# Preactivation convolutions with a mixture block, one core: the order of stores, halos, scales and PSUM banks in the last four steps

## The chip, the cores and the metric

The kernel runs on one core of one Trainium2 chip. The metric is the device time of one execution in microseconds (us), median of three: 566.34 us (565.69 to 567.6). Differences of about 0.3% (1.7 us) or less can't be told from no change here.

## The reference, cut to what matters

Four layers, each added to its input; the group norm has 4 groups of 2 channels over the whole image, so no element of a layer can be normalised before the last of its image is known.

```python
# x: (4, 8, 256, 256) float32: four images of eight channels
def _gn(v, G=4, eps=1e-05):
    g = v.reshape(B_, G, C_ // G, H_, W_)
    m = jnp.mean(g, axis=(2, 3, 4), keepdims=True)
    s = jnp.var(g, axis=(2, 3, 4), keepdims=True)
    return ((g - m) / jnp.sqrt(s + eps)).reshape(v.shape)
x = x + _L0_conv_ref(_gn(x), L0_conv_weight, L0_conv_bias)     # 3x3 convolution, 8 to 8 channels, padding 1
x = x + _L1_conv_ref(_gn(x), L1_conv_weight, L1_conv_bias)
x = x + _L2_conv_ref(_gn(x), L2_conv_w1, L2_conv_b1, L2_conv_w2, L2_conv_b2)
#   h = gelu(einsum('bend,edf->benf', x, w1) + b1); einsum('benf,efd->bend', h, w2) + b2, one pair of matrices per channel
x = x + _L3_conv_ref(_gn(x), L3_conv_weight, L3_conv_bias)
```

## The kernel before, in words

**Tiling.** An image is held as 128 partitions (column parity, channel, row within a band of 8) by 4096 columns (32 bands of 128 column pairs), in float32 in `X`. It is worked on in 8 chunks of 512 columns, one PSUM bank each. The convolutions are twelve steps: 0 to 3 the first layer on images 0 to 3, 4 to 7 the second, 8 to 11 the last (images 0 to 3). The gated matrices (L2) lie between step 7 and step 8.

**One step of a convolution.** GpSimd (`scale_and_bias`) turns the image's variance into a scale and a bias per partition. ScalarE (`normalise_piece`) writes the normalised piece twice: as float16 into `XN` and as float32 into `SCR`; GpSimd (`low_part`) subtracts the two into the low half of `XN`. An image has five pieces (2, 2, 1, 1, 2 chunks). The rows above and below a band belong to other partitions, so DMAs copy them from `XN` to `HALO`: for each half of an image four transfers of `halo_columns` and four of `halo_thirds`. TensorE computes the part within a band (`centre`, 3 matmuls for each chunk) and then, for four chunks at a time, the sides and halos (`tiles`: 48 matmuls on quarters of the array, in two halves of 24, first those signalled as `cross_mm`, then those as `conv_mm`). VectorE adds the bank to `X` (`conv_update`). The four `conv_update`s of a half of an image in the last layer give output, stored by DMAs from `X` to `out`.

**Statistics.** The means and variances within a partition come from VectorE (`bn_stats`, `bn_aggr`). Across the partitions of a group, two tiny TensorE matmuls sum them: `group_mean(n)`, then VectorE's `deviation(n)`, then `group_variance(n)`, then VectorE's `variance(n)`, which lets GpSimd make the scale. The last layer has n = 12 to 15 for images 0 to 3.

**The last layer.** The results of the matrices for images 2 and 3 are transposed on TensorE (`results(b, first, last)`) and added by VectorE (`mlp_chunk`) in the same stretch in which steps 8 and 9 run, so that image 3's statistics are complete only within step 9. The order on each engine is written out by hand; there is no scheduler. `ORDER` lists in which order the chunks of `X` become final, and semaphore waits are counted from it. `L3_BANKS` gives the PSUM bank of each of the 32 chunks of the last layer. `XN` and `HALO` have three slots; step 11 uses the slot of step 8. SP and ScalarE each have a DMA queue, which they fill in program order: whatever SP waits for, all its later transfers wait too.

## Time and profile before

| | |
|---|---|
| time, median of 3 | 566.34 us (565.69 to 567.6) |
| the profiled execution | 566.28 us |
| its span, first to last instruction | 564.5 us |
| TensorE busy, share of the span | 515.9 us, 91% |
| VectorE, ScalarE, GpSimd busy | 372.4 us, 295.7 us, 170.5 us |
| moved by DMA | 57.41 MB, mean 102 GB/s |
| output written | 8.39 MB |

The span is 1.8 us shorter than the time of its execution; the rest lies around it. A busy share is a mean over the whole program. In the last 45 us it says little: there the engines take turns, and it counts which wait ends last. Times in the rows below are microseconds from the span's start. In a timeline each row is an instruction or several merged ones; what stands in brackets is how long the engine was idle before it and what ended that.

### The profile page before, as it was taken

How to read it: one execution, taken by the hardware profiler on the slowest of the kernel's cores; microseconds unless marked ns; L12 is line 12 of the kernel's file. 1: busy time of each engine (PE TensorE's matmuls, PEld its weight loads, DVE VectorE, ACT ScalarE, POOL GpSimd, SP SyncE). 2: the span in 40 equal slices, each digit the busy share in tenths (PEclk: the TensorE clock that was granted, in tenths of full speed). 3: DMA queues.
4: the chain of work that ended last, by engine and by line, in shares of the span. 5: the costliest groups of instructions: out<-in, count | busy, mean ns of one | idle time of the engine just before them, and what ended most of it. 6: DMA issues, size and time to landing. Idle time of an engine off the chain costs nothing.

```text
span 564.5 us, 9154 instructions
## 1 busy us (share of the span) xinstructions
PE 515.9 (91%) x3374; PEld 259.3 (46%) x3374; DVE 372.4 (66%) x637; ACT 295.7 (52%) x363; POOL 170.5 (30%) x188
## 2 busy tenths in 40 slices
PE   0779999996989999999999999999999989998874
PEld 0434444563544444444444444444444445864431
DVE  4889999987866394194193293292358388898523
ACT  2699988553734453353353362352346646886430
POOL 4679888886470000000000000000000000587430
PEclk9799999997899999999999999999999999999988
DMA  8845655543020221021022012012132300054778
GB/s 318 345 109 144 155 136 137 134 124 150 1 75 1 75 75 75 0 74 74 0 74 74 2 73 74 10 64 74 35 115 75 138 12 2 1 133 109 241 229 330
DMA packets 14168, 57.41 MB, mean 102 GB/s; under 512 B 3116, under 2 KB 3244, under 8 KB 11052
## 3 DMA queue, kind: packets, MB, share of 16 engines
q1 hardware_dynamic: 12396, 51.39, 28.5%
q10 hardware_dynamic: 1740, 5.58, 2.8%
q8 instruction: 21, 0.34, 0.3%
q14 instruction: 11, 0.09, 0.0%
HBM read 30.03 MB, written 8.39 MB: 68 GB/s over the span
## 4 chain that ended last, share of the span: by engine, by line
PE 61%; DVE 16%; ACT 7%; POOL 5%; DMA 3%; SPq 3%; issue 3%; ACTq 0%; DVEq 0%; POOLq 0%
PE PS L1097 26%; PE PS L1071 25%; DVE X L735 6%; DVE ST L696 5%; PE PS L973 3%; SPq L262 3%; POOL XN L384 3%; ACT SCR L494 2%; ACT XN L489 2%; PE PS L1028 2%; DMA X<-x 2%; DMA HALO<-XN 2%; PE PS L1127 2%; PE PS L966 1%; DVE SM L711 1%
## 5 line engine op out<-in xcount | busy, mean ns | idle before, releaser
L1071 PE MATMUL PS<-XT,W1S 128*128 (+1 forms) x768 | 171.7, 382 | 2.8 <-POOL XT L433 2.5
L1097 PE MATMUL PS<-HID,W2S 128*128 128x512 f16 x720 | 159.5, 379 | 1.6 <-DVE W2S L760 1.6
L535 ACT ACTIVATE SCR<-PS,CONST 128x512 f32<-128x512 f32 x128 | 87.2, 687 | 64.5 <-PE PS L1071 28.0
L1071 PEld LDWEIGHTS PS<-XT,W1S 128*128 128x128 f16 x768 | 75.5, 99 | 92.2 <-issue 5.9
L1097 PEld LDWEIGHTS PS<-HID,W2S 128*128 128x128 f16 x720 | 70.4, 98 | 82.9 <-issue 1.8
L384 POOL TENSOR_TENSOR XN<-SCR,XN 128x1024 f16<-128x1024 f32 (+1 forms) x61 | 100.5, 1671 | 24.3 <-ACT SCR L494 24.1
L760 DVE SCALAR_TENSOR_TENSOR W2S<-W2F,W2S 128x2048 f16<-128x2048 f32 x10 | 22.9, 2291 | 114.6 <-ACT W2S L531 114.6
L361 POOL MEMSET XN<- 128x128 f16 x6 | 2.8, 460 | 304.3 <-PE PS L1097 304.0
L696 DVE BATCH_NORM_STATS2 ST<-X 128x6 f32<-128x512 f32 x128 | 81.6, 682 | 9.4 <-DMA X<-x 8.2
L489 ACT ACTIVATE XN<-X,SC 128x1024 f16<-128x1024 f32 (+1 forms) x61 | 64.2, 1052 | 32.1 <-POOL SC L375 23.2
L973 PE MATMUL PS<-XN,CWT 64*64 64x512 f16 x288 | 68.5, 385 | 8.1 <-DMA HALO<-XN 8.1
L735 DVE SCALAR_TENSOR_TENSOR X<-PS,X 128x512 f32<-128x512 f32 x96 | 59.6, 680 | 22.9 <-PE PS L988 22.9
L966 PE MATMUL PS<-XN,CWT 128*128 128x512 f16 x288 | 68.8, 385 | 2.8 <-DVE X L735 1.4
L807 DVE SCALAR_TENSOR_TENSOR HID<-SCR,HID 128x512 f16<-128x512 f32 x96 | 67.4, 702 | 3.3
L986 PE MATMUL PS<-HALO,CWT 49*64 49x512 f16 (+1 forms) x288 | 68.9, 385 | 0.0
L988 PE MATMUL PS<-HALO,CWT 49*64 49x512 f16 (+1 forms) x288 | 68.9, 385 | 0.0
L975 PE MATMUL PS<-XN,CWT 64*64 64x512 f16 x288 | 68.5, 385 | 0.0
L494 ACT ACTIVATE SCR<-X,SC 128x1024 f32<-128x1024 f32 (+1 forms) x61 | 64.1, 1050 | 2.5 <-POOL XN L384 1.9
L561 ACT ACTIVATE YT<-PS,CONST 128x512 f32 (+1 forms) x24 | 16.5, 688 | 88.7 <-PE PS L1097 88.7
L804 DVE TENSOR_SCALAR HID<-SCR 128x512 f16<-128x512 f32 x96 | 40.8, 425 | 9.5 <-ACT SCR L535 6.4
L973 PEld LDWEIGHTS PS<-XN,CWT 64*64 64x64 f16 x288 | 29.3, 108 | 37.5 <-DMA HALO<-XN 11.0
L966 PEld LDWEIGHTS PS<-XN,CWT 128*128 128x128 f16 x288 | 27.3, 100 | 36.8 <-issue 4.8
(52 smaller groups left out, 482.4 us busy)
## 6 DMA issues: line engine op xcount, KB each, us to landing
W1F<-w SPq DMA_DIRECT2D x10, 1024.0 KB, 4.8
W2F<-w SPq DMA_DIRECT2D x10, 1024.0 KB, 4.8
HALO<-XN SPq DMA_DIRECT2D x48, 129.9 KB
HALO<-XN SPq DMA_DIRECT2D x48, 121.8 KB
X<-x SPq DMA_DIRECT2D x2, 2048.0 KB, 18.8
out<-X ACTq DMA_DIRECT2D x8, 512.0 KB, 5.2
HALO<-XN SPq DMA_DIRECT2D x42, 64.9 KB
HALO<-XN SPq DMA_DIRECT2D x42, 60.9 KB
```

The lines of the kernel that those rows point to most:

```text
L384: pool.tensor_tensor(XN[s][:, 1, rows, 1:NJ + 1], SCR[:, m % 2, 0:n * CH].rearrange("p (t j) -> p t j", j=NJ), XN[s][:, 0, rows, 1:NJ + 1] ...
L489: act.activation(XN[s][:, 0, i * TC:(i + n) * TC, 1:NJ + 1], src.rearrange("p (t j) -> p t j", j=NJ), ACT.Identity, bias=SC[:, k, 1:2], sc ...
L494: act.activation(SCR[:, m % 2, 0:n * CH], src, ACT.Identity, bias=SC[:, k, 1:2], scale=SC[:, k, 0:1]).then_inc(xn_ok, 1)
L535: act.activation(SCR[:, ft % 2, 0:CH], bank(ft % G_RING), ACT.Gelu, bias=BT[:, ds(e * FT + ft, 1)], scale=1.0 / (XS * WS)).then_inc(gelu_o ...
L696: dve.bn_stats(ST[:, n % 4, slot], src).then_inc(bn_ok, 1)
L735: dve.scalar_tensor_tensor(out=xc, in0=bank(conv_bank(q)), scalar=1.0 / (XS * WS), in1=xc, op0=ALU.mult, op1=ALU.add).then_inc(x_new, 1)
L966: pe.matmul(to, CWT[:, w, l, 0:P], XN[s][:, part, rows, 1:NJ + 1], start=(n == 0), stop=False)
L973: odd = pe.matmul(bank(k, HALF_P, P), CWT[0:HALF_P, w, l, SIDE:EDGE], XN[s][0:HALF_P, part, rows, 2:NJ + 2], start=False, stop=last)
L986: even = pe.matmul(bank(k, 0, HALF_P), CWT[0:kh, w, l, EDGE:CWN], HALO[s][0:kh, part, rows, 0:NJ], start=False, stop=last)
L988: odd = pe.matmul(bank(k, HALF_P, P), CWT[HALF_P:HALF_P + kh, w, l, EDGE:CWN], HALO[s][HALF_P:HALF_P + kh, part, rows, 0:NJ], start=False, ...
L1071: mm = pe.matmul(bank(ft % G_RING), W1S[:, w, h * NF + ft * P:h * NF + (ft + 1) * P], rhs, start=(n == 0), stop=(n == 3 * DH - 1))
L1097: mm = pe.matmul(bank(G2_BANK + h), W2S[:, w, ft * NW + h * P:ft * NW + (h + 1) * P], HID[slot][:, part, ft], start=(ft == 0 and part == 0 ...
```

## The change

It touches the last four steps alone. On SP, stores (512 KB transfers from `X` to `out`) now stand between the halo transfers: two of image 0 between the two halves of step 9's halos and two behind them, then step 10's halos, then four stores of image 1 and two of image 2, then step 11's halos. ScalarE no longer issues image 0's stores; it issues the thirds of step 10 (`last_thirds(10, ...)`) and those of step 11 after all five pieces of the step, and image 2's second half and part of image 3's stores at the end. GpSimd makes image 2's scale (`scale_and_bias(14)`) before the last piece of step 9. On TensorE the sums of n = 14 and 15 are issued in the middle of `tiles`, and the last two results of image 3 come earlier. VectorE takes up the last result of image 3 after two of step 9's updates. `L3_BANKS` uses up to eight banks.

```diff
-L3_STAT_BANK = 2
+L3_STAT_BANK = (2, 6)
-L3_BANKS = [(3, 4, 5, 0, 1)[n % 5] for n in range(2 * NCH)]
-L3_BANKS += [(6, 7, 4, 5, 0, 1, 3)[n % 7] for n in range(2 * NCH)]
+L3_BANKS = [3, 4, 5, 0, 1, 3, 4, 5, 0, 1, 2, 3, 4, 5, 0, 1]
+L3_BANKS += [(7, 6, 2, 3, 4, 5, 0, 1)[n % 8] for n in range(2 * NCH)]
-THIRDS_BY_ACT = ((0, 0), (11, 0), (11, 1),)
+THIRDS_BY_ACT = ((0, 0), (10, 0), (10, 1), (11, 0), (11, 1))
@@ SP
-        for g in range(8, 11):
-            load_ones(SLOT[g])
-            halos(g)
-        for i in range(0, NCH, 2):
-            sp.wait_ge(x_new, X_NEW_AT["c", 9, i + 1])
-            sp.dma_start(out[1][:, i * CH:(i + 2) * CH], x_chunk(1, i, 2)
-                         ).then_inc(out_done, 16)
+        def store(b, i, n=2):
+            sp.wait_ge(x_new, X_NEW_AT["c", 8 + b, i + n - 1])
+            sp.dma_start(out[b][:, i * CH:(i + n) * CH], x_chunk(b, i, n)).then_inc(out_done, 16)
+        def store_half(b, i):
+            store(b, i)
+            store(b, i + 2)
+        load_ones(SLOT[8])
+        halos(8)
+        load_ones(SLOT[9])
+        halos(9, lambda: store_half(0, 0))      # called between the two halves of the halos
+        store_half(0, QUAD)
+        load_ones(SLOT[10])
+        halos(10)
+        store_half(1, 0)
+        store_half(1, QUAD)
+        store_half(2, 0)
         halos(11)
-        for i in range(NCH):
-            sp.wait_ge(x_new, X_NEW_AT["c", 11, i])
-            sp.dma_start(out[NB - 1][:, i * CH:(i + 1) * CH], x_chunk(NB - 1, i)
-                         ).then_inc(out_done, 16)
+        store(NB - 1, 0)
+        store(NB - 1, 4, 1)
+        store(NB - 1, 6, 1)
@@ GpSimd
-        low_parts(9)
+        low_parts(9, 0, 4)
+        scale_and_bias(14)
+        low_parts(9, 4)
...
-        for g in range(10, 12):
-            scale_and_bias(g + 4)
-            low_parts(g)
+        low_parts(10)
+        scale_and_bias(15)
+        low_parts(11)
@@ ScalarE
-        for g in range(9, 11):
+        for g in range(9, 12):
             normalise(g)
-        store(0)
-        slot_free(11)
-        for k in range(4):
-            normalise_piece(FIRST_PIECE[11] + k)
-        last_thirds(0)
-        normalise_piece(FIRST_PIECE[11] + 4)
-        last_thirds(1)
-        store(2)
+            if g >= 10:
+                last_thirds(g, 0)
+                last_thirds(g, 1)
+        store(2, 4)
+        store(2, 6)
+        store(NB - 1, 2)
+        store(NB - 1, 5, 1)
+        store(NB - 1, 7, 1)
@@ TensorE, banks of the last layer
-                elif L3_BANKS[n] >= TR_BANK:
-                    pe.wait_ge(x_new, X_NEW_AT["y", 3, 6 + L3_BANKS[n] - TR_BANK])
+                elif L3_BANKS[n] in L3_STAT_BANK:
+                    pe.wait_ge(var_ok, 2 * (15 + L3_STAT_BANK.index(L3_BANKS[n])))
+                elif L3_BANKS[n] == TR_BANK + 1:
+                    pe.wait_ge(x_new, X_NEW_AT["y", 3, NCH - 1])
@@ TensorE, order
-        tiles(8, 0)
-        group_mean(14)
+        tiles(8, 0, lambda: group_mean(14))
...
-        tiles(9, 0)
-        results(3, 6, 6)
+        tiles(9, 0, lambda: results(3, 6, 6))
+        results(3, 7, 7)
         last_centres(9, 4, 7)
-        results(3, 7, 7)
-        tiles(9, QUAD, lambda: group_mean(15))
-        group_variance(15)
+        group_mean(15)
+        tiles(9, QUAD, lambda: group_variance(15))
```

On VectorE, in the first half of step 9's updates up to image 3's variance (L735, now L749, is a `conv_update`; L753, now L767, adds a result, and L696, now L710, takes its statistics; L701 to L719, now L715 to L733, are the aggregate, deviation and variance), before:

```order
L735 SCALAR_TENSOR_TENSOR X<-PS,X 128x512 x4
L753 TENSOR_TENSOR X<-PS,X 128x512
L696 BN_STATS ST<-X 128x6
L701 BN_AGGR MV<-ST 128x2
L707 TENSOR_TENSOR SM<-MV,PS 128x1
L709 TENSOR_SCALAR SM<-PS 128x1
L711 SCALAR_TENSOR_TENSOR SM<-SM,MV 128x1
L717 TENSOR_SCALAR SM<-PS 128x1
L719 TENSOR_SCALAR SM<-PS 128x1
L735 SCALAR_TENSOR_TENSOR X<-PS,X 128x512 x20
```

and now:

```order
L749 SCALAR_TENSOR_TENSOR X<-PS,X 128x512 x2
L767 TENSOR_TENSOR X<-PS,X 128x512
L710 BN_STATS ST<-X 128x6
L715 BN_AGGR MV<-ST 128x2
L749 SCALAR_TENSOR_TENSOR X<-PS,X 128x512
L721 TENSOR_TENSOR SM<-MV,PS 128x1
L723 TENSOR_SCALAR SM<-PS 128x1
L725 SCALAR_TENSOR_TENSOR SM<-SM,MV 128x1
L749 SCALAR_TENSOR_TENSOR X<-PS,X 128x512
L731 TENSOR_SCALAR SM<-PS 128x1
L733 TENSOR_SCALAR SM<-PS 128x1
L749 SCALAR_TENSOR_TENSOR X<-PS,X 128x512 x20
```

The last result of image 3 moved ahead of two of the four updates, which now stand where VectorE had nothing between the steps of the statistics.

On SP's queue, step 10's halos and what follows them (`HALO_57` is step 10's slot), before:

```order
L318 DMA HALO_57<-ones 2x4160 [waits zero_ok2]
L262 DMA HALO_57<-XN_56 16x2x1948 [waits zero_ok2,lo_ok,pads_ok2,conv_mm]
L262 DMA HALO_57<-XN_56 16x2x1948
L262 DMA HALO_57<-XN_56 16x2x2078 x2
L262 DMA HALO_57<-XN_56 8x2x1948 x2
L262 DMA HALO_57<-XN_56 8x2x2078 x2
L262 DMA HALO_57<-XN_56 16x2x2078 [waits lo_ok]
L262 DMA HALO_57<-XN_56 16x2x2078
L262 DMA HALO_57<-XN_56 16x2x1948 x2
L262 DMA HALO_57<-XN_56 8x2x2078 x2
L262 DMA HALO_57<-XN_56 8x2x1948 x2
L344 DMA out<-X 128x1024 [waits x_new] x4
```

and now (with the first of step 11's, `HALO_54`):

```order
L344 DMA out<-X 128x1024 [waits x_new] x2
L321 DMA HALO_57<-ones 2x4160 [waits zero_ok2]
L263 DMA HALO_57<-XN_56 16x2x1948 [waits zero_ok2,lo_ok,pads_ok2,conv_mm]
L263 DMA HALO_57<-XN_56 16x2x1948
L263 DMA HALO_57<-XN_56 16x2x2078 x2
L263 DMA HALO_57<-XN_56 16x2x2078 [waits lo_ok]
L263 DMA HALO_57<-XN_56 16x2x2078
L263 DMA HALO_57<-XN_56 16x2x1948 x2
L344 DMA out<-X 128x1024 [waits x_new] x6
L263 DMA HALO_54<-XN_52 16x2x1948 [waits zero_ok0,lo_ok,pads_ok0,conv_mm]
```

The eight transfers of eight rows have left this queue for ScalarE's, two stores stand ahead of step 10's halos, and six instead of four between them and step 11's.

## Rows read from the trace of the kernel before

**Rows 1.** Busy time by stretch; columns: stretch, its length, each engine, clock, DMA.

```profile
core 0: us, PE busy (x) PEld busy (x) DVE busy (x) ACT busy (x) POOL busy (x), PEclk, DMA share, GB/s
...
536.00:542.00 6.00, 6.00 (x64) 2.77 (x63) 3.02 (x6) 2.18 (x3) 3.56 (x3) 1.00 0.98 362
...
547.00:550.40 3.40, 3.40 (x36) 1.52 (x36) 0.00 (x0) 0.00 (x0) 0.25 (x1) 0.50 0.49 95
```

**Rows 2.** Timeline of TensorE, 519 to 566 us.

```profile
521.95 2.15 PE L966 MATMUL PS<-XN,CWT 128*128 128x512 f16 x9 [1.45 <-DVE X L735]
...
526.45 0.38 PE L931 MATMUL PS<-MV,CONST 128*128 128x1 f32 x2 [0.49 <-DVE MV L701]
...
528.44 2.79 PE L966 MATMUL PS<-XN,CWT 128*128 128x512 f16 x12
532.16 0.40 PE L973 MATMUL PS<-XN,CWT 64*64 64x512 f16 x1 [0.93 <-DMA HALO<-XN]
...
540.36 2.80 PE L966 MATMUL PS<-XN,CWT 128*128 128x512 f16 x12
546.88 0.56 PE L973 MATMUL PS<-XN,CWT 64*64 64x512 f16 x1 [3.72 <-DMA HALO<-XN]
...
551.29 2.80 PE L966 MATMUL PS<-XN,CWT 128*128 128x512 f16 x12
```

**Rows 3.** Timeline of VectorE, 506 to 559 us.

```profile
506.95 0.14 DVE L719 TENSOR_SCALAR SM<-PS 128x1 f32<-128x1 f32 x1
...
519.89 0.69 DVE L753 TENSOR_TENSOR X<-PS,X 128x512 f32<-128x512 f32 x1 [1.53 <-PE PS L1044]
...
524.57 0.69 DVE L753 TENSOR_TENSOR X<-PS,X 128x512 f32<-128x512 f32 x1 [0.88 <-PE PS L1044]
...
528.61 0.16 DVE L717 TENSOR_SCALAR SM<-PS 128x1 f32<-128x1 f32 x1 [1.26 <-PE PS L936]
...
556.29 2.48 DVE L735 SCALAR_TENSOR_TENSOR X<-PS,X 128x512 f32<-128x512 f32 x4 [2.97 <-PE PS L988]
```

**Rows 4.** Timeline of GpSimd, 507 to 525 us.

```profile
507.38 2.06 POOL L384 TENSOR_TENSOR XN<-SCR,XN 128x1024 f16<-128x1024 f32 x1 [1.03 <-ACT SCR L494]
...
511.09 0.56 POOL L368 TENSOR_TENSOR RS<-SM,RS 128x1 f32<-128x1 f32 x1
...
517.50 4.24 POOL L384 TENSOR_TENSOR XN<-SCR,XN 128x1024 f16<-128x1024 f32 x3 [0.18 <-ACT SCR L494]
522.78 2.06 POOL L384 TENSOR_TENSOR XN<-SCR,XN 128x1024 f16<-128x1024 f32 x1 [1.03 <-ACT SCR L494]
```

**Rows 5.** Timeline of ScalarE, 508 to 554 us.

```profile
512.78 1.25 ACT L489 ACTIVATE XN<-X,SC 128x1024 f16<-128x1024 f32 x1 [5.48 <-POOL SC L375]
...
530.60 1.25 ACT L489 ACTIVATE XN<-X,SC 128x1024 f16<-128x1024 f32 x1 [7.89 <-POOL SC L375]
```

**Rows 6.** Timeline of SP's queue, 505 to 562 us.

```profile
505.35 10.41 SPq L262 DMA_DIRECT2D HALO<-XN  x16
...
535.56 3.21 SPq L344 DMA_DIRECT2D out<-X  x4
538.93 11.08 SPq L262 DMA_DIRECT2D HALO<-XN  x8
```

**Rows 7.** The chain that ended last, 519 to 566 us.

```profile
520.77 0.61 SPq L262
...
522.40 2.39 SPq L262
...
529.70 2.42 DMA HALO<-XN
...
542.82 4.01 DMA HALO<-XN
```

**Rows 8.** All stores from X to out, by tile.

```profile
L349 SPq DMA_DIRECT2D out<-X x8: 332/1166/1218, 551.6 to 559.9; - x8
...
DMA to landing us min/median/max: 3.1/5.0/7.8
```

More of the change, by code:

```diff
@@ L89 @@
 ORDER += [("c", 8, i) for i in range(QUAD, NCH)] + [("y", 3, i) for i in range(3, 7)]
-ORDER += [("c", 9, i) for i in range(QUAD)] + [("y", 3, 7)]
-ORDER += [("c", 9, i) for i in range(QUAD, NCH)]
+ORDER += [("c", 9, 0), ("c", 9, 1), ("y", 3, 7)]
+ORDER += [("c", 9, i) for i in range(2, NCH)]
 ORDER += [("c", g, i) for g in range(10, 12) for i in range(NCH)]
@@ L190, in stat_psum @@
     def stat_psum(n, col):
-        k = 0 if n == 13 else L3_STAT_BANK if n > 13 else STAT_BANK
+        k = 0 if n == 13 else L3_STAT_BANK[n - 14] if n > 13 else STAT_BANK
         return PS[:, k * CH + col:k * CH + col + 1]
@@ L298, in _, with halos @@
         load_image(3, 0, NT, x3_in)
-        def halos(g):
+        def halos(g, between=None):
             s = SLOT[g]
@@ L309, in halos @@
                 halo_thirds(sp, s, 0, NT // 2, halo_a[s])
+            if between is not None:
+                between()
             sp.wait_ge(lo_ok, PIECE_OF[g, NCH - 1] + 1)
@@ L338, in _ @@
             load_w2(e)
-        for g in range(8, 11):
-            load_ones(SLOT[g])
-            halos(g)
-        for i in range(0, NCH, 2):
-            sp.wait_ge(x_new, X_NEW_AT["c", 9, i + 1])
-            sp.dma_start(out[1][:, i * CH:(i + 2) * CH], x_chunk(1, i, 2)
-                         ).then_inc(out_done, 16)
-        halos(11)
-        for i in range(NCH):
-            sp.wait_ge(x_new, X_NEW_AT["c", 11, i])
-            sp.dma_start(out[NB - 1][:, i * CH:(i + 1) * CH], x_chunk(NB - 1, i)
-                         ).then_inc(out_done, 16)
-        sp.wait_ge(out_done, 16 * (NPR * (NB - 1) + NCH))
+        def store(b, i, n=2):
[14 more added lines that the diff above has]
+        store_half(2, 0)
+        halos(11)
+        store(NB - 1, 0)
+        store(NB - 1, 4, 1)
+        store(NB - 1, 6, 1)
+        sp.wait_ge(out_done, 16 * (NPR * NB + 2))
     @block.gpsimd
@@ L664, in _, with store, last_thirds @@
             last_result(1, dh)
-        def store(b):
-            for i in range(0, NCH, 2):
-                act.wait_ge(x_new, X_NEW_AT["c", 8 + b, i + 1])
-                act.dma_start(out[b][:, i * CH:(i + 2) * CH], x_chunk(b, i, 2)
-                              ).then_inc(out_done, 16)
-        def last_thirds(half):
-            s = SLOT[11]
+        def store(b, i, n=2):
+            act.wait_ge(x_new, X_NEW_AT["c", 8 + b, i + n - 1])
+            act.dma_start(out[b][:, i * CH:(i + n) * CH], x_chunk(b, i, n)
+                          ).then_inc(out_done, 16)
+        def last_thirds(g, half):
+            s = SLOT[g]
             act.wait_ge(pads_ok[s], 2)
             act.wait_ge(zero_ok[s], 4)
-            act.wait_ge(conv_mm, 2 * NCH * (HAD[11] + 1))
-            act.wait_ge(lo_ok, PIECE_OF[11, NCH - 1 if half else QUAD] + 1)
+            act.wait_ge(conv_mm, 2 * NCH * (HAD[g] + 1))
+            act.wait_ge(lo_ok, PIECE_OF[g, NCH - 1 if half else QUAD] + 1)
             halo_thirds(act, s, half * NT // 2, (half + 1) * NT // 2, (halo_a, halo_b)[half][s])
-        for g in range(9, 11):
+        for g in range(9, 12):
             normalise(g)
-        store(0)
-        slot_free(11)
-        for k in range(4):
-            normalise_piece(FIRST_PIECE[11] + k)
-        last_thirds(0)
-        normalise_piece(FIRST_PIECE[11] + 4)
-        last_thirds(1)
-        store(2)
+            if g >= 10:
[6 more added lines that the diff above has]
+        store(NB - 1, 7, 1)
     @block.vector
@@ L908, in _ @@
             mlp_chunk(3, i)
-        last_updates(9, 0, None)
+        conv_update(9, 0)
+        conv_update(9, 1)
         mlp_chunk(3, 7)
         aggregate(15)
+        conv_update(9, 2)
         deviation(15)
+        conv_update(9, 3)
         variance(15)
@@ L928, in group_mean @@
                 pe.wait_ge(yt_ok, 4 * NE + 2)
+            elif n == 15:
+                pe.wait_ge(x_new, X_NEW_AT["y", 3, 6])
             elif n >= 1:
```

## The prediction

> **What bounds the kernel now.** I read four views. The busy time by stretch comes first: nothing that the change touches lies ahead of 502 us, so only the last 62 us can move. TensorE is at full clock there except from 547.0 to 550.4 us, where the granted clock is 0.50, its lower level of 1.2 GHz; just before that it had stood idle [rows 1, 2]. The timeline of TensorE then shows which waits it has: 1.45 us for an update by VectorE (a PSUM bank is not free), 0.49 us for image 3's aggregate, 0.93 us for the first halos of step 10 and 3.72 us for the first halos of step 11 [rows 2]. Everything between them is matmuls back to back: four `centre`s take 2.73 us and a full `tiles` as much (from 532.16 to 540.36 there are three such blocks and no gap [rows 2]). Third, who is late behind the halos: ScalarE sits idle 5.48 us before step 10 and 7.89 us before step 11, each time for the scale [rows 5]. GpSimd makes image 2's scale at 511.09, only after the last piece of step 9 (507.38) [rows 4], though VectorE had the variance at 507.1; it can make image 3's only after VectorE has read that variance at 528.61 [rows 3]. Fourth, the queue: SP issues a halo transfer every 0.65 us (16 in 10.41 us) when the DMA engines are free [rows 6], but 2.39 us for one when 2 MB of stores run beside it [rows 7]. Before step 11 its four stores of image 1 (2 MB) go ahead of the halos; these start at 538.93 (the stores at 535.56), TensorE gets them at 546.88, 7.95 us later, with the DMA engines 98% busy from 536 to 542 [rows 1, 2, 6]. After the last update ends (556.29 + 2.48 = 558.77) the span runs another 5.7 us on stores [rows 3].
>
> **The change part by part.** I carry the starts of instructions, since matmul ends overlap.
>
> Step 8. The mean of image 2 moves into `tiles`. It has to wait there for the aggregate by some 0.5 us; but TensorE waited about as long afterwards for VectorE's deviation, which doesn't move. I take 0; from -0.3 to +0.5 (the 0.49 of the same kind of wait [rows 2]).
>
> Step 9, TensorE. Chunk (9,5) took bank 0 from (9,0), whose update VectorE began only after the result (3,6). With bank 2 put in, (9,6) is the first chunk to need it, one `centre` (0.69) later; and the result (3,6) comes half a `tiles` (1.3 us) earlier, so VectorE can begin it at about 518.5 instead of 519.89 [rows 3] and (9,0) at 519.8 instead of 521.2. TensorE reaches (9,6) at 521.6, so that wait goes, 1.45 us, 1.5 with the refilling of the pipeline. The aggregate: 518.5, plus 1.3 for the result and its statistics, 1.25 for two updates and 1.83 for the last result, its statistics and the aggregate (524.57 to the mean's matmul at 526.45 [rows 2, 3], less its start) gives 522.9. TensorE gets to the mean at 522.9 as well, so the second wait (0.49, with the refilling 0.6) goes too. Step 10's centres begin 2.1 us earlier, at 526.3. Bounds: 0.6, if the bank wait only moves to the mean, to 2.3.
>
> Image 3's scale. The variance's matmul is now in the middle of `tiles`, at 523.0 + 0.3 + 1.3 = 524.6; VectorE reads it 0.4 later, at 525.0, against 528.61 [rows 3]. The two updates that stand between don't delay it: the deviation waits for the mean until 523.4 and one update (0.6) fits on each side. GpSimd is free by then, so everything behind the scale moves 3.6 us: ScalarE starts step 11 at 527.0 instead of 530.60 [rows 5].
>
> Image 2's scale. It goes ahead of step 9's last piece, so it can start once GpSimd has piece four and the variance, at 507.2 (506.95 + 0.14 [rows 3]; piece four is done at 506.4, where GpSimd's idle 1.03 us begin) instead of 511.09. It takes 1.7 us, from 511.09 to ScalarE's start at 512.78 [rows 4, 5]. What it pushes back is that piece (507.38 to 509.1), the memsets behind it, and step 9's second halos by 0.6 us; TensorE needs these only at 523, and SP issues them by 519 (below). ScalarE starts step 10 at 509.1 instead of 512.78. GpSimd is busy with the delayed piece (2.06) and 1.6 us of memsets (509.4 to 511.0 now) until 512.8 and passes on 2.5 us of it: the piece that step 10's first halos wait for (the second of three at 517.50 [rows 4]) is ready at 518.2 instead of 520.7, the last at 522.3 instead of 524.8.
>
> SP's queue. Step 9's first eight halos end at 510.6 as now. Two stores (1 MB) cost 1.3 us to issue, the eight second halos 5.2 us plus 1.1 for the stores beside them (beside 2 MB eight issues, the first at 520.77 and the last at 529.70, took 8.9 us between them instead of 7 x 0.65, 4.3 more [rows 7]; I take a quarter of that for half the data, and a half as the bound). Two more stores and the ones: 520.2. Step 10's four column halos, 2.5 + 1.1 us, are issued by 523.8 and land by about 526.3 (the last one's issue to landing was 2.42 us [rows 7]). The four thirds, which leave this queue, go out on ScalarE's at 518.1 to 521. TensorE wants them at 526.3 + 2.73 = 529.0. So the wait of 0.93, 1.0 with the refilling, goes, with 2.7 us to spare. Of the stores, image 1's are out by 530; image 2's first two wait for updates at 532.5 and 533.7.
>
> Step 11's halos. SP began them at 538.93, as soon as the piece was ready; 3.6 to 3.9 us earlier is 535.0 to 535.3. SP has just issued the second of image 2's stores and reaches the halos at 535.1; 1 MB is ahead of them instead of 2 MB, and ScalarE issues its thirds at the same time and not before a piece that it still has to normalise. Four issues with 1.1 extra begin the last at 538.1 (now four from 538.93 begin the last at 542.82, 3.89 us [rows 6, 7]; this is 3.0); at 2.42 us for landing it is there at 540.6. TensorE is ready at 526.3 + 5 x 2.73 = 540.0. I take a wait of 0.6 us instead of 3.8 with the refilling, a gain of 3.2. Bounds: no wait (gain 3.8), or 7.95 us from start to landing as now, 543.1, a wait of 3.1 (gain 0.7).
>
> Clock. The first `tiles` of step 11 took 546.88 to 551.29, 4.41 us instead of 2.73, since 3.4 us of it ran at 0.50 [rows 1, 2]. Waits of 1.45 and 0.93 us left the clock at 1.00 and 3.72 us did not. With 0.6 us I count the 1.7 us as gained; all of it stays lost if the wait is near 3.7.
>
> End. Of image 3's second half, SP and ScalarE each issue two 256 KB stores; now SP issues eight in a row at 1.17 us each, the last at 559.9, 1.2 us after its update was done [rows 3, 8]. Also 2 MB of image 2 no longer drains at the same time; only 1 MB of it, 6 us earlier. The last store now took 4.1 us to land; the least of all stores is 3.1 us [rows 8]. I take 3.7: 5.7 becomes 0.05 + 3.7 + 0.4 = 4.15, a gain of 1.6; bounds 1.2 and 2.2.
>
> The Trainium skill (Trainium Kernel Development and Optimization, Key Constraints) says that DMAs from SP and ScalarE run on the same 16 engines and that issuing from several only saves the sequencer's issue time. By that rule alone the end would give 1.2 us and not 1.6, and the sum would be 557.0. This trace has both queues busy at once in its last 10 us and can't tell saved issue from saved transfer.
>
> **The sum.** 2.1 (step 9) + 1.0 (step 10's halos) + 3.2 (step 11's) + 1.7 (clock) + 1.6 (end) = 9.6 us. The profiled execution took 566.28, which is the median of 566.34 but for 0.06: 566.3 - 9.6 = 556.7; I forecast **556.7 us**, a span of 554.9. Its own range is 554.6 to 559.0.
>
> **The rivals.**
>
> A. The stores hold the halos as long as now. What counts is then not the 2 MB but that stores stand directly ahead on one queue: step 11's halos take the 7.95 us again, land at 543.1, TensorE waits 3.1 us and its clock falls as now. 2.5 us and 1.7 us of the gain are lost: 560.9. For it: the landing took 4.01 us behind 2 MB [rows 7], and six stores now stand ahead of these halos. Against it: four of them will have drained.
>
> B. A halo's completion follows all earlier stores. A store takes up to 7.8 us to land [rows 8]; if the halos' signal can't be earlier than that of the store issued at 533.7, it comes at 541.5 to 542, 1.2 us after my value: 557.9. The Trainium skill (DMA: Bandwidth & Descriptors, Queues, rings and completion order) has such a rule: the semaphore increment lands only after every earlier write of its DMA engine, across queues. By it ScalarE's queue would be no way round the stores. The trace has no halo landing before a store issued ahead of it that it could be held against.
>
> C. Image 3's scale is no earlier: VectorE, not TensorE, is the bound of step 9, and the updates put between the statistics cost what they save. The variance stays near 528; halos of step 11 start at 538.9 on empty queues, land at 543.4: 561.2. Against it are VectorE's three gaps of 1.53, 0.88 and 1.26 us there [rows 3].
>
> D. Slower. SP is one chain now: step 10's halos behind four stores. If the stretched prices hold for each (8.9 + 0.6 us for the eight second halos of step 9, 3.9 + 0.9 for four of step 10, 4.0 to land [rows 6, 7]) they come at 532.7 instead of 526.3. Past 532.1, today's arrival, nothing is won there; TensorE idles 3.8 us and loses 1.7 us of clock; update (10,3) and so image 2's second store move to 539.7, and step 11's halos, queued behind that store, take their 7.95 us from 541: 549.0, against 546.88 now, with the clock lost again. Less 1.6 at the end: 567 to 568. It takes all prices at their worst at once.
>
> E. The halos keep TensorE waiting as before and only the end is gained: 564.7 to 566, within 0.3%.
>
> **How the numbers follow.** Forecast 0.62, A 0.17, B 0.09, C 0.05, D 0.04, E 0.03. The range from 554.6 to 561.3 leaves out D, E and the tails of the others, together about 0.15. 0.3% is 1.7 us, about what a measurement tells from no change. Faster: all of the first four, 0.93; same, E and a share of D, 0.03; slower 0.04.
>
> **What would show it.** TensorE: no wait before the three centres of step 9, step 10's centres at 526 and its `tiles` at 529 with no idle time, step 11's first `tiles` at 540 to 541 after under 1.5 us, no stretch at 0.50 before the last update. GpSimd: scale of image 2 at 507.2, of image 3 at 525 to 525.5. SP: step 10's first halo at 520 to 521, step 11's at 535. Last update's end to span's end: 4.2 us. I am wrong if a wait of over 3 us for halos remains in step 10 or 11, if image 3's scale begins after 527, or if the end still takes 5.7 us.

## The result, and the profile after

The changed kernel takes 556.38 us (median of 4, 555.54 to 560.05) against 566.36 us (565.69 to 567.6, 4 runs) of the kernel before on the same chip: a ratio of 0.9829, 95% interval 0.9803 to 0.9855, or 9.98 us faster. The forecast was 556.7 us. The profiled execution took 555.82 us with a span of 554.0 us, against 566.28 and 564.5. One execution of run 9 below (1091.39 us) and one of the kernel before beside runs 1 to 4 (1091.97 us) took about twice as long as all others and are in no ratio.

TensorE's timeline from 515 us on, to be laid beside [rows 2]:

```profile
520.18 2.79 PE L988 MATMUL PS<-XN,CWT 128*128 128x512 f16 x12
526.25 2.80 PE L988 MATMUL PS<-XN,CWT 128*128 128x512 f16 x12
531.72 2.80 PE L988 MATMUL PS<-XN,CWT 128*128 128x512 f16 x12
537.18 2.80 PE L988 MATMUL PS<-XN,CWT 128*128 128x512 f16 x12
541.04 0.40 PE L995 MATMUL PS<-XN,CWT 64*64 64x512 f16 x1 [1.05 <-DMA HALO<-XN]
543.77 2.80 PE L988 MATMUL PS<-XN,CWT 128*128 128x512 f16 x12
```

Of the four waits of before one is left, 1.05 us before step 11's first `tiles`. Step 10's centres start at 526.25 (528.44 before); from there to 537.18 blocks follow each other every 5.47 us, so the halos of step 10 are in time. VectorE, GpSimd and ScalarE around the two scales, beside [rows 3 to 5] (one fence for each engine):

```profile
519.71 1.27 DVE L749 SCALAR_TENSOR_TENSOR X<-PS,X 128x512 f32<-128x512 f32 x2
...
548.77 2.48 DVE L749 SCALAR_TENSOR_TENSOR X<-PS,X 128x512 f32<-128x512 f32 x4 [2.98 <-PE PS L1010]
```

```profile
506.96 0.56 POOL L381 TENSOR_TENSOR RS<-SM,RS 128x1 f32<-128x1 f32 x1 [0.82 <-DVE SM L733]
...
525.23 0.56 POOL L381 TENSOR_TENSOR RS<-SM,RS 128x1 f32<-128x1 f32 x1 [3.60 <-DVE SM L733]
```

```profile
508.64 1.24 ACT L504 ACTIVATE XN<-X,SC 128x1024 f16<-128x1024 f32 x1 [1.55 <-POOL SC L388]
...
526.91 1.24 ACT L504 ACTIVATE XN<-X,SC 128x1024 f16<-128x1024 f32 x1 [7.42 <-POOL SC L388]
```

Both scales start on VectorE's variance and on nothing else: image 2's at 506.96 (511.09 before), image 3's at 525.23; ScalarE starts step 11 at 526.91 instead of 530.60. SP's queue, beside [rows 6]:

```profile
518.02 1.09 SPq L344 DMA_DIRECT2D out<-X  x2
519.17 0.82 SPq L321 DMA_DIRECT2D HALO<-ones  x1
520.15 6.35 SPq L263 DMA_DIRECT2D HALO<-XN  x8
526.55 3.44 SPq L344 DMA_DIRECT2D out<-X  x4
532.57 1.53 SPq L344 DMA_DIRECT2D out<-X  x2
534.86 6.79 SPq L263 DMA_DIRECT2D HALO<-XN  x8
```

Image 1's 2 MB are issued from 526.55 to 530.0; the first of them stands eight microseconds before step 11's halos, the last some five. The DMA engines are far from idle in between. The next two lines show it, with the DMA share and GB/s as their last two numbers:

```profile
532.00:534.00 2.00, 2.00 (x11) 0.91 (x10) 1.73 (x3) 1.94 (x4) 2.00 (x2) 1.00 0.96 377
534.00:536.00 2.00, 2.00 (x33) 0.91 (x35) 0.00 (x0) 2.00 (x3) 1.86 (x2) 1.00 1.00 399
```

By the packets of the trace (those of 4,096 bytes are the stores' alone), image 1's stores end at 533.9 and image 2's first two at 537.4, after the first halo transfer of step 11 has been issued. Now the chain that ended last, beside [rows 7], and all stores, beside [rows 8]:

```profile
534.94 0.63 ACTq L263
...
536.30 0.70 ACTq L263
537.03 3.96 DMA HALO<-XN
541.04 0.40 PE PS L995
```

```profile
L344 SPq DMA_DIRECT2D out<-X x13: 332/430/1155, 510.4 to 550.7; - x13
L683 ACTq DMA_DIRECT2D out<-X x5: 338/338/1274, 542.1 to 551.3; - x5
...
DMA to landing us min/median/max: 2.2/4.3/6.2
```

Last, the busy time by stretch, beside [rows 1]: the granted clock is 1.00 where it was 0.50.

```profile
530.00:536.00 6.00, 6.00 (x78) 2.75 (x70) 2.48 (x4) 5.94 (x8) 5.67 (x4) 1.00 0.99 395
536.00:542.00 6.00, 4.95 (x56) 2.17 (x52) 2.48 (x4) 0.80 (x1) 2.07 (x1) 1.00 0.82 205
...
547.00:550.40 3.40, 2.31 (x44) 1.10 (x36) 1.63 (x3) 0.00 (x0) 0.00 (x0) 1.00 0.67 270
```

Where the 10.5 us between the two spans come from, by starts: 2.2 up to step 10's centres (528.44 to 526.25; 0.2 of it this execution was ahead by before step 9); 1.0 at step 10's first `tiles` (3.72 us after the centres before, 2.73 now); 2.7 at step 11's (6.52 us after its centres, now 3.86); 1.7 in the clock (4.41, now 2.73); 3.0 at the end (from the last update's end to the span's end 5.7, now 554.0 - 551.25 = 2.7).

### The profile page after: what moved, and what is told of

It reads as the page before. It is cut to its first block, busy times and chain, and to the rows that moved or that the text cites. A ratio compares the mean times of both kernels' runs of the same rounds, so it can differ in the third digit from the quotient of the medians.

```text
span 554.0 us, 9155 instructions
## 1 busy us (share of the span) xinstructions
PE 514.7 (93%) x3374; PEld 258.8 (47%) x3374; DVE 371.8 (67%) x637; ACT 295.3 (53%) x363; POOL 170.2 (31%) x188
## 4 chain that ended last, share of the span: by engine, by line
PE 64%; DVE 18%; ACT 6%; POOL 4%; DMA 3%; issue 3%; SPq 1%; ACTq 1%; DVEq 0%; POOLq 0%
PE PS L1119 27%; PE PS L1093 26%; DVE X L749 6%; DVE ST L710 6%; PE PS L995 3%; PE PS L988 2%; POOL XN L397 2%; PE PS L1050 2%; ACT SCR L509 2%; DMA X<-x 2%; ACT XN L504 2%; PE PS L1066 2%; PE PS L1149 1%; DVE X L767 1%; DVE SM L725 1%
## 5 line engine op out<-in xcount | busy, mean ns | idle before, releaser
L710 DVE BATCH_NORM_STATS2 ST<-X 128x6 f32<-128x512 f32 x128 | 81.6, 681 | 9.2 <-DMA X<-x 8.0
L749 DVE SCALAR_TENSOR_TENSOR X<-PS,X 128x512 f32<-128x512 f32 x96 | 59.7, 680 | 19.1 <-PE PS L1010 19.0
L995 PE MATMUL PS<-XN,CWT 64*64 64x512 f16 x288 | 67.1, 378 | 4.4 <-DMA HALO<-XN 4.4
L1008 PE MATMUL PS<-HALO,CWT 49*64 49x512 f16 (+1 forms) x288 | 67.6, 378 | 0.0
L1010 PE MATMUL PS<-HALO,CWT 49*64 49x512 f16 (+1 forms) x288 | 67.6, 378 | 0.0
L997 PE MATMUL PS<-XN,CWT 64*64 64x512 f16 x288 | 67.1, 378 | 0.0
```

The costliest lines, as they stand in the source:

```text
L710: dve.bn_stats(ST[:, n % 4, slot], src).then_inc(bn_ok, 1)
L749: dve.scalar_tensor_tensor(out=xc, in0=bank(conv_bank(q)), scalar=1.0 / (XS * WS), in1=xc, op0=ALU.mult, op1=ALU.add).then_inc(x_new, 1)
L995: odd = pe.matmul(bank(k, HALF_P, P), CWT[0:HALF_P, w, l, SIDE:EDGE], XN[s][0:HALF_P, part, rows, 2:NJ + 2], start=False, stop=last)
L1008: even = pe.matmul(bank(k, 0, HALF_P), CWT[0:kh, w, l, EDGE:CWN], HALO[s][0:kh, part, rows, 0:NJ], start=False, stop=last)
L1010: odd = pe.matmul(bank(k, HALF_P, P), CWT[HALF_P:HALF_P + kh, w, l, EDGE:CWN], HALO[s][HALF_P:HALF_P + kh, part, rows, 0:NJ], start=False, ...
```

## The experiments

In each the number that matters is how long step 11's first halo copies (the halo transfers of before, for the first half of the image) take, from SP's first issue to TensorE's start. It is collected in a table behind the last experiment. Each such time comes from one profiled execution, and the spread between executions has to be kept in mind: run 7 has the instructions of the changed kernel up to these copies and needs 6.8 us where the changed kernel needs 6.2; the kernel before and runs 3 and 4, which are equal up to there too, need 7.95, 7.9 and 8.0.

**1 and 2. Order and queues apart.** One kernel has the changed queues (stores, thirds) with the order of before (banks, sums, result, scales); the other the reverse.

The first, against the changed kernel:

```diff
-L3_STAT_BANK = (2, 6)
+L3_STAT_BANK = 2
-        low_parts(9, 0, 4)
-        scale_and_bias(14)
-        low_parts(9, 4)
+        low_parts(9)
...
-        tiles(9, 0, lambda: results(3, 6, 6))
+        tiles(9, 0)
+        results(3, 6, 6)
```

and the second:

```diff
-THIRDS_BY_ACT = ((0, 0), (10, 0), (10, 1), (11, 0), (11, 1))
+THIRDS_BY_ACT = ((0, 0), (11, 0), (11, 1),)
-        halos(9, lambda: store_half(0, 0))
...
+        for g in range(8, 11):
+            load_ones(SLOT[g])
+            halos(g)
+        for i in range(0, NCH, 2):
+            sp.wait_ge(x_new, X_NEW_AT["c", 9, i + 1])
```

> The engines' order, the scales and the banks are those of before; SP's and ScalarE's queues (stores between halos, thirds of step 10, the split end) are the new ones. Theory (the terms add up, queue by queue): step 10's halos no longer make TensorE wait (1.0 us), step 11's halos start at 538.5 as before and take 6.1 us to arrive (as in the changed kernel, 534.86 to 541.0) instead of 7.95, so the wait is 2.5 instead of 3.8 (1.3 us), the end gains 3.0 us, and the clock's 1.7 us come back only if a wait of 2.5 us leaves it at full speed: 561.0, or 559.3 with the clock. Rival (the stores only help together with the earlier scales, because without them they stand in the way of the halos): 564 to 566.

> The engines' order, the scales and the banks are the new ones; SP's and ScalarE's queues are those of before. Theory: step 9 gives its 2.0 us and image 3's scale comes at 525.2, but SP issues image 1's 2 MB only at about 533, directly ahead of step 11's halos, and these take 7.95 us from 536.3: 544.2, while TensorE is ready at 540.6. The wait stays 3.6 us, the clock falls, the end is as before: 563.7. Rival (the earlier scales carry the change and the queues hardly matter): below 560.

Measured: 560.75 us (ratio 0.9895, 0.9871 to 0.9919) and 562.63 us (0.9939, 0.992 to 0.9958); before 566.04. So the order alone gives 3.4 us and the queues alone 5.3, together 8.7, and both at once 9.98. TensorE's rows of the first and of the second:

```profile
540.76 2.80 PE L977 MATMUL PS<-XN,CWT 128*128 128x512 f16 x12
546.15 0.40 PE L984 MATMUL PS<-XN,CWT 64*64 64x512 f16 x1 [2.59 <-DMA HALO<-XN]
548.88 2.80 PE L977 MATMUL PS<-XN,CWT 128*128 128x512 f16 x12
```

```profile
543.05 0.63 PE L986 MATMUL PS<-XN,CWT 64*64 64x512 f16 x1 [3.22 <-DMA HALO<-XN]
...
550.62 0.40 PE L986 MATMUL PS<-XN,CWT 64*64 64x512 f16 x1 [0.44 <-DMA HALO<-XN]
```

With a late scale but spread stores the copies take 6.2 us (539.96 to 546.15); a wait of 2.6 us leaves the clock alone. With an early scale but four stores right ahead they take 7.6 us (535.46 to 543.05), and a stretch of 3.4 us from 543.0 runs at a granted clock of 0.51.

**3. The end alone.** The kernel before, with image 3's stores split between SP and ScalarE as in the changed kernel.

```diff
-        for i in range(NCH):                               # SP: eight stores of 256 KB
+        for i, n in ((0, 2), (4, 1), (6, 1)):              # SP
...
+        for i, n in ((2, 2), (5, 1), (7, 1)):              # ScalarE, at its end
```

> The kernel before with one edit: image 3's stores are split over both queues as in the changed kernel (SP: chunks 0-1, 4, 6; ScalarE: 2-3, 5, 7, behind image 2's four stores). Theory: of the 3.0 us that the end gained, 1.2 are saved issue time and 1.8 come from image 2's 2 MB no longer draining beside it; so this gives 1.2 us: 565.2. Rival (the split alone makes the end): 3.0 us, 563.4.

Measured: 566.79 us (1.0013, 0.9997 to 1.0029), no change. Stretches of it around the last update's end (558.7):

```profile
550.00:558.70 8.70, 6.16 (x72) 2.61 (x64) 4.88 (x8) 0.00 (x0) 0.00 (x0) 1.00 0.98 362
558.70:564.40 5.70, 0.00 (x0) 0.00 (x0) 0.01 (x1) 0.00 (x0) 0.00 (x0) 0.64 0.73 281
```

The last store is issued at 558.74 instead of 559.94, so the second queue does save 1.2 us of issue, and the span still runs 5.7 us on. The DMA engines are 98% busy before the last update's end, and 1.6 MB are moved after it (5.7 us at 281 GB/s). The same stretch in the kernel before and in the changed kernel:

```profile
558.80:564.50 5.70, 0.00 (x0) 0.00 (x0) 0.00 (x0) 0.00 (x0) 0.00 (x0) 0.66 0.73 277
```

```profile
551.20:554.00 2.80, 0.00 (x0) 0.00 (x0) 0.06 (x1) 0.00 (x0) 0.00 (x0) 0.97 0.69 258
```

That is 1.6 MB before and 0.7 MB now. The end waits for bytes, not for issue.

**4. The clock alone.** The kernel before, with 15 more matmuls into a free bank (their results are not used) ahead of step 11's first `tiles`, so that TensorE hardly stands still (0.29 us are left).

```diff
+                if (g, i) == (11, 0):
+                    for _ in range(15):
+                        pe.matmul(bank(2), CWT[:, 0, 2, 0:P], XN[SLOT[11]][:, 0, 0:TC, 1:NJ + 1],
+                                  start=True, stop=True)
```

> The kernel before with 15 matmuls of 512 columns into the unused bank 2 put into TensorE's wait for step 11's first halos (15 x 0.216 = 3.2 us in an idle time of 3.72). Their result is not read. Theory: the granted clock stays at 1.00 and the first tiles of step 11 take 2.73 instead of 4.41 us: 1.7 us faster, 564.6. Rival (the clock's fall costs nothing here, since the stores set the end anyway): 566.3.

Measured: 566.61 us (1.0002, 0.9985 to 1.002). The clock stayed at 1.00 and the block took 2.73 us, but the last `tiles` then stood 1.84 us for step 11's *second* copies, whose thirds ScalarE issued only after its last piece, and began at 554.11 (554.02 in the kernel before). The 1.7 us of the clock are worth nothing while those are late.

**5 and 6. The last piece before the thirds.** The kernel before, with ScalarE normalising all five pieces of step 11 before it issues thirds, without and with the matmuls of experiment 4.

```diff
-        for k in range(4):
+        for k in range(5):
             normalise_piece(FIRST_PIECE[11] + k)
         last_thirds(0)
-        normalise_piece(FIRST_PIECE[11] + 4)
         last_thirds(1)
```

> The kernel before with one edit: ScalarE normalises all five pieces of step 11 before it issues the thirds of its halos (before, the fifth piece stood behind the first four thirds and was ready at 547.25). Theory (the last 10 us are bound by 4 MB that drain after 550 us): image 2's stores now start near 545.5 instead of 550.1, so that only image 3's 2 MB are left at the end and each of its stores takes some 0.34 us to issue; TensorE's last tiles stay at 554.0, since the first ones still run at the lower clock. 2 to 2.9 us faster: 563.5. Rival (the end is bound by eight issues in a row on one queue, which this leaves as they are): 566.

> As e5, with the 15 unread matmuls in TensorE's wait before step 11's first tiles. Theory: the second halos are no longer late, so the clock's 1.7 us, which the run with the matmuls alone lost again in a wait of 1.9 us for them, now reach the end: 1.7 us faster than e5, 561.8. Rival (the second halos are late for another reason, the stores on the queues): as e5.

Measured: 564.21 us (0.9964, 0.9946 to 0.9981) and 562.47 us (0.9938, 0.9918 to 0.9958). Now the clock does give its 1.7 us (the medians of one chip; the two intervals overlap a little): it needed the second copies in time. Run 5's trace shows two effects of the fifth piece. With it out of the way, image 2's four stores are issued from 544.47 to 549.0 and not from 550.09 to 554.2, and the end takes 2.8 us from the last update and not 5.7, with 0.7 MB moved in it and all of image 3's stores still on SP's queue. That is the end's gain in full, without a second queue. But the first copies take 9.3 us and not 7.95 (9.4 in run 6), TensorE stands 5.07 us and its clock is at 0.50 for 6.8 us and not 3.4, so that only 1.8 us are left. This part of the change (five pieces, then the thirds) was in the diff, and the prediction gave it half a sentence.

**7. The end on one queue.** The changed kernel with image 3's eight stores all on SP again.

```diff
-        store(NB - 1, 0)
-        store(NB - 1, 4, 1)
-        store(NB - 1, 6, 1)
+        for i in range(NCH):
+            store(NB - 1, i, 1)                            # and none on ScalarE
```

> The changed kernel with one edit: all of image 3 is stored by SP again, in eight stores of 256 KB; the rest as changed. Theory (issues are slow only when data is waiting to drain; here 0.34 us each, less than an update of 0.6): no change, 556.4. Rival (the split saves the issue time of 1.2 us, as forecast): 557.6.

Measured: 556.48 us (0.9844, 0.9818 to 0.9871), as the changed kernel. Each of SP's last four issues takes 0.33 us; in the kernel before the last three took 1.05 to 1.21. The 1.2 us that the prediction took for issue time was backlog too.

**8 and 9. Image 2's first two stores elsewhere.** In the changed kernel they stand ahead of step 11's copies; here between their halves (8) and behind both (9).

```diff
-        store_half(2, 0)
-        halos(11)
+        halos(11, lambda: store_half(2, 0))                # 8
+        halos(11); store_half(2, 0)                        # 9
```

> The changed kernel with one edit: SP issues image 2's first two stores between the two halves of step 11's halos, not ahead of them. Theory (1 MB ahead in the queue holds the halos up): the wait of 1.05 us for the first halos goes, 555.4. Rival (the halos take 4 us to land for their own sake): 556.4; and if the second halos come too late for it, TensorE waits there instead.

> The changed kernel with image 2's first two stores issued behind both halves of step 11's halo copies, not ahead of them; the rest as it was. In the run with the stores between the halves, the copies issued ahead of the stores took 7.1 us from the first issue to TensorE's start (533.12 to 540.21), where the changed kernel's took 6.2 (534.86 to 541.04) with the stores ahead. Theory: what is issued within a few microseconds behind the copies shares the 16 engines with them and slows them as much as what is ahead, so only stores that start after the copies have landed are free; here they start at about 541 to 543, by when the first copies have landed: the first tiles of step 11 start without the 1.05 us wait, the second copies land in time, and the stores themselves add to the end, where 0.4 MB/us is moved already. I expect 556.0 us (0.4 less than the changed kernel, 1.05 gained and about 0.6 given back at the end). Rival (a store behind the copies can't slow them; the run between the halves lost its time to the second copies): 555.3. Rival (1 MB more in the queues at the end costs its full 2.6 us): 558.

Measured: 558.03 us (0.9864, 0.984 to 0.9888) and 558.24 us (0.9864, 0.9844 to 0.9884; the median of three executions), neither better than the changed kernel. They are 1.7 and 1.9 us slower by the medians, but their intervals overlap a little with the changed kernel's (0.9803 to 0.9855), so that this isn't clear of noise. TensorE in 8 and in 9:

```profile
540.21 0.40 PE L994 MATMUL PS<-XN,CWT 64*64 64x512 f16 x1 [1.95 <-DMA HALO<-XN]
544.62 2.81 PE L987 MATMUL PS<-XN,CWT 128*128 128x512 f16 x12
```

```profile
540.74 0.40 PE L995 MATMUL PS<-XN,CWT 64*64 64x512 f16 x1 [1.01 <-DMA HALO<-XN]
543.48 2.80 PE L988 MATMUL PS<-XN,CWT 128*128 128x512 f16 x12
```

and the stretches of 9 before the copies, during them and after the last update:

```profile
532.00:534.60 2.60, 2.60 (x19) 1.06 (x21) 1.48 (x3) 2.54 (x5) 2.60 (x3) 1.00 0.47 183
534.60:540.70 6.10, 5.13 (x59) 2.23 (x48) 2.48 (x4) 1.96 (x2) 3.07 (x2) 1.00 0.62 151
```

```profile
551.00:556.00 5.00, 0.00 (x0) 0.00 (x0) 0.00 (x0) 0.00 (x0) 0.00 (x0) 0.72 0.65 250
```

My theory for 9 fell. With no store within 5 us ahead and the DMA engines half idle the copies took 6.13 us, against 6.18 with 1 MB ahead: two stores ahead are free, and some 6.1 us are what the copies take by themselves. The stores came back at the end, 5.0 us instead of 2.7, which is what the second rival (558) said. In 8 the copies took 7.09 us and the clock was lost (4.41 us for the block) although the stores were issued behind the first four copies of their queue; run 7's 6.8 us without any such store is close to it, so that this delay is not shown to be the stores'. Neither place is better than the changed kernel's.

**10 and 11. Step 10's thirds on SP again; image 2's scale late again.** I had priced these two parts of the change together at the 1.0 us of step 10's wait.

```diff
-THIRDS_BY_ACT = ((0, 0), (10, 0), (10, 1), (11, 0), (11, 1))        # 10
+THIRDS_BY_ACT = ((0, 0), (11, 0), (11, 1),)
-            if g >= 10:
+            if g >= 11:
...
-        low_parts(9, 0, 4)                                          # 11
-        scale_and_bias(14)
-        low_parts(9, 4)
+        low_parts(9)
...
         zero_pads(2, 1)
+        scale_and_bias(14)
```

> The changed kernel with the thirds of step 10's copies issued by SyncE again, 16 in a row, not half by ScalarE. In the changed kernel SyncE's copies start at 520.15 and TensorE needs the first at 528.98 without a wait; the thirds cost SyncE some 3 to 4 us more, of which 2.3 stand before the first landing by the kernel before (16 in 10.41 us). Theory, as the prediction put it, that the halos of step 10 are in time by about 2.7 us: the move of the thirds is worth 0 to 0.6 us: 556.7. It also pushes image 1's stores on SyncE back by some 3 us, which the backlog before step 11's copies could feel: up to 1 us more. Rival (the thirds are what made step 10's copies timely): 558.5 or more.

> The changed kernel with image 2's scale put back behind the whole of step 9's low parts on GpSimd, where it stood before. GpSimd then gets to it some 3.8 us later (the last four of the low parts), ScalarE's normalisation of image 2 moves by as much, and step 10's copies with it: 523.9 in place of 520.15, landing about 6 to 7 us later at 530 to 531, where TensorE wants the first at 528.98. Theory: the wait of 0.9 to 1.0 us at step 10's first tiles returns, and the later copies of step 10 crowd the stores of image 1 and step 11's copies: 557.5 us. Rival (slack of 2.7 us is enough, the scale's place is worth nothing): 556.4.

Measured: 564.61 us (0.9962, 0.9948 to 0.9976) and 560.68 us (0.9878, 0.986 to 0.9896). Taken back alone, the thirds cost 8.2 us of the 10 and the scale 4.3. Neither run waits at step 10: its centres and the next stand 5.47 and 5.46 us apart. SP's queue and TensorE in 10:

```profile
531.96 5.83 SPq L344 DMA_DIRECT2D out<-X  x6
537.95 9.59 SPq L263 DMA_DIRECT2D HALO<-XN  x8
```

```profile
532.43 2.80 PE L988 MATMUL PS<-XN,CWT 128*128 128x512 f16 x12
548.14 0.63 PE L995 MATMUL PS<-XN,CWT 64*64 64x512 f16 x1 [7.44 <-DMA HALO<-XN]
```

SP is with the copies of step 10 until 531.9, so image 1's four stores go out together with image 2's two right before step 11's copies, and these take 10.2 us. In 11 step 10's last four copies begin at 524.52 and not 523.81, image 1's stores at 527.34 and not 526.55; image 2's two stores take 0.68 and 1.57 us to issue at 532.62 and 533.82 (0.33 each in the changed kernel), and the copies take 9.4 us. The stores ahead are the same six as in the changed kernel, nearly as early: their last packet ends 4.5 us after the first copy was issued, and 2.6 us after it there. Why that is followed by 3.2 us more for the copies is open. The profiled execution of 11 is also the slowest of its five (562.28 us; the others 558.44 to 560.7), so its trace shows more than the 4.3 us, among it a clock at 0.50 for 6.8 us.

**12. The stores bunched, nothing else.** The changed kernel with one wait more on SP.

```diff
         halos(10)
+        sp.wait_ge(x_new, X_NEW_AT["c", 10, 1])
         store_half(1, 0)
```

> The changed kernel with one wait more: SyncE begins image 1's four stores only when the second update of image 2 is in X (532.5 in the changed kernel's trace, where they went out at 526.55 to 530.0), so that all six stores (3 MB) stand right before step 11's halo copies; no queue, no scale and no other order is touched. It is the state of the run with step 10's thirds on SyncE (six stores at 531.96 to 537.79, copies from 537.95 to TensorE's start at 548.14, 10.2 us) without its cause. Theory: the gain of the change hangs on the stores being drained before step 11's copies start; with them bunched the copies start at about 536.5 to 538 and take 9.5 to 10.2 us (6.2 in the changed kernel), TensorE starts at 546.5 to 548 and not 541.04, the clock halves for one stretch: 562.5 to 564.5. Rival (the copies take 6.2 us whatever was stored just before, and the run with the thirds lost its time to their issue on SyncE): start at 536, TensorE at 542.2, 557.6.

Measured: 565.16 us (0.9988, 0.997 to 1.0006): all of the gain is gone. SP's queue and TensorE:

```profile
534.17 5.79 SPq L344 DMA_DIRECT2D out<-X  x6
540.12 11.22 SPq L263 DMA_DIRECT2D HALO<-XN  x8
```

```profile
549.04 0.63 PE L996 MATMUL PS<-XN,CWT 64*64 64x512 f16 x1 [7.44 <-DMA HALO<-XN]
553.14 2.80 PE L989 MATMUL PS<-XN,CWT 128*128 128x512 f16 x12
```

Nothing that computes was touched and step 10's thirds are still ScalarE's; the state of experiment 10 is there, with the same idle time of 7.44 us. The rival (a fixed 6.2 us) is out. But not all of the loss is slower copies. This execution was 1.6 us behind the changed kernel's before step 11 (533.32 against 531.72 for the last four centres of step 10). Past that, SP comes to the copies 3.7 us later, since it has waited and then issued six stores in 5.8 us; the copies take 2.7 us longer and the clock costs 1.4. In run 10 the same sum is 2.4 us later, 4.0 longer and 1.5 for the clock.

Step 11's first copies in all kernels, what SP had stored before them, and how long after the first copy's issue the last packet of these stores ends (from the packets of each trace):

| kernel | stores ahead | their last packet, after the first issue | first issue to TensorE's start |
|---|---|---|---|
| 9 | none in 5 us | 0.4 before it | 534.61 to 540.74: 6.1 |
| changed | 2 (1 MB), and 4 issued by 530.0 | 2.6 | 534.86 to 541.04: 6.2 |
| 1 | 2, and 4 by 533.3 | 0.2 | 539.96 to 546.15: 6.2 |
| 7 | as changed | 3.5 | 534.66 to 541.48: 6.8 |
| 8 | none in 4.7 us; 2 behind the first four | 0.1 | 533.12 to 540.21: 7.1 |
| 2 | 4 (2 MB) | 4.2 | 535.46 to 543.05: 7.6 |
| 3 | 4 | 3.5 | 538.22 to 546.15: 7.9 |
| before | 4 | 4.1 | 538.93 to 546.88: 7.95 |
| 4 | 4 | 3.7 | 538.71 to 546.72: 8.0 |
| 12 | 6 (3 MB) | 5.1 | 540.12 to 549.04: 8.9 (ScalarE's thirds from 536.52: 12.5) |
| 5 | 4, all thirds at once | 4.1 | 537.52 to 546.82: 9.3 |
| 11 | 2, and 4 by 532.0 | 4.5 | 535.55 to 544.96: 9.4 |
| 6 | 4, all thirds at once | 4.6 | 538.52 to 547.94: 9.4 |
| 10 | 6 | 5.3 | 537.95 to 548.14: 10.2 (ScalarE's thirds from 535.65: 12.5) |

Stores that still run 2.6 us into the copies cost nothing; where they run on 3.5 us or more the copies take 6.8 to 10.2 us. The number of stores alone doesn't order the rows. Within the rows of 4.1 to 4.6 us there is a second difference, which no run changes alone: in 5, 6 and 11 the copies of the second half are issued while the first are still under way (4.2 to 5.1 us after the first issue), and the first take 9.3 us or more; in 2 and before they come only after these have landed (8.3 us or later), and it is 7.95 us or less.

## Why the prediction was right

**Step 9** (2.1 forecast): 2.0. TensorE's two waits and VectorE's first gap went at the places named; step 10's centres came at 526.25 (526.3 forecast).

**Image 3's scale**: 525.23, forecast 525 to 525.5. **Image 2's**: 506.96, forecast 507.2.

**Step 10's halos** (1.0): 1.0, and the slack forecast (2.7 us) is at least in part there: run 10, with the thirds on SP again, has no wait here either. Run 11's copies of step 10 start only 0.3 us later than the changed kernel's and say little of it. But the prediction saw the value of the thirds' move and of image 2's scale here, and it isn't here. Without the thirds' move SP comes to image 1's stores 5.4 us later (531.96 against 526.55), right before step 11's copies, and run 12 brings about the same by a wait alone. Runs 10 to 12 show 8.2, 4.3 and 8.8 us for three edits of which each alone keeps the rest of the change. These are not shares and needn't add up to 10: 10 and 12 spoil the same thing. That the scale works by the same path is argued only, since run 11 delays image 1's stores by just 0.8 us.

**Step 11's halos** (3.2 forecast, bounds 0.7 to 3.8): 2.7. The wait was 1.05 and not 0.6. The landing of the last copy, 3.96 us, was mis-sized: I took the 2.42 us of step 10 [rows 7]; it is a third of ScalarE's that comes last. Run 9 shows that this is no remainder of the stores, since it stays without them. The bound of 0.7 us of gain (7.95 us again) was not reached; the forecast of fewer bytes ahead was right in its direction.

**Clock** (1.7): 1.7. The step was right only with a condition that the prediction didn't name: the second copies have to come earlier as well (runs 4 to 6). They do, since the fifth piece no longer waits behind the thirds: SP issues them from 538.97 on and not from 547.27.

**End** (1.6 forecast, bounds 1.2 to 2.2): 3.0, the term that was mis-sized, outside its bounds. I took 1.2 us of it as issue time saved by a second queue, and 3.7 us for the last store's landing, which is over within the 2.7 us from its issue (551.29) to the span's end. Run 3 (second queue, old backlog: nothing) and run 7 (one queue, new backlog: as good) show that the number of queues is worth nothing on either side; it is the bytes that still drain after the last update, 1.6 MB before and 0.7 MB now, and run 5 brings them down to 0.7 MB by image 2's earlier stores, with one queue. The Trainium skill (Trainium Kernel Development and Optimization, Key Constraints) grants several issuers the saving of issue time only; run 3 had that saving, 1.2 us, and ended no earlier.

The sum 9.6 stood against 9.98 measured and 10.5 between the profiled spans: 1.4 too little at the end and 0.5 too much at step 11. That the total came nearer than its terms is luck: two errors of opposite sign, and a difference of the medians that lies 0.5 us below that of the two traces.

**Rivals.** A (what counts is that stores stand directly ahead) is refuted in its form by the changed kernel, 6.2 us with two stores directly ahead; but its price is real where they run on longer (6.8 to 10.2 us in the table). B (a halo's completion follows all earlier stores) gave 541.5 to 542 for TensorE's start; it was 541.04, and 540.74 with no store near. Whether the 9 to 10 us of runs 10 and 12 come from completion order, as the Trainium skill (DMA: Bandwidth & Descriptors, Queues, rings and completion order) would have it, or from shared transfer, no run here tells apart. C is out by the scale at 525.23. D had the right mechanism, late stores held ahead of step 11's copies, at a price that didn't arise: run 10 is what it would have looked like, and ends within 0.4% of before. E is out.

Open: why the copies take 6.1 us when all stores have landed (run 9), of which some 2.6 us are the four issues; why the copies of runs 5 and 6 take 9.3 and 9.4 us behind four stores where the kernel before needs 7.95 (in them the copies of both halves follow each other at once); why run 11's take 9.4.

## What to carry to other kernels

A large transfer that nobody waits for should be gone before a small one that somebody waits for begins: not by a place in the order alone, but by several microseconds (here 2 MB issued at 526.5 and not at 535.5). A sign in a trace is the issue time of the last store ahead: 0.33 to 0.40 us where the copies took 6.2 to 6.8 us (changed kernel, runs 1 and 7), 0.85 to 1.63 us where they took 7.6 or more. It is no proof of an empty queue: in the changed kernel it was 0.33 us with the DMA engines 96% busy, and at the end of run 9 the last stores took 0.33 to 0.45 us to issue and the span ran on for 5.0 us. An edit is to be priced also by what its queue does next, not only by the wait it was made for. An edit that seems to have slack may hold most of the gain; delay one transfer on purpose to find out.
